# Stages between the Mamba scans merged into one stage by groups of four sequences, and the same for combine, norm and feed-forward

## What is computed

```python
def _mamba(x, wi, cw, cb, xpw, dw, db, Alog, Dp, wo):
    xin, z = jnp.split(jnp.einsum('bld,ed->ble', x, wi), 2, axis=-1)
    u = _silu(cb + sum((xpad[:, k:k + Ls, :] * cw[:, k] for k in range(4))))
    dt_in, Bc, Cc = split(jnp.einsum('blc,ec->ble', u, xpw))
    dt = jax.nn.softplus(jnp.einsum('blr,cr->blc', dt_in, dw) + db)
    ys = scan over 128 steps of h = exp(dt * A) * h + dt * u * B, y = h . C
    return jnp.einsum('blc,dc->bld', (ys + u * Dp) * _silu(z), wo)
for i in range(3):
    m = _layernorm(m + _mamba(m, ...), ln_g[i], ln_b[i])
moe_out = mix + shared
ff_out = silu(layer_norm(moe_out) @ ff_w1 + ff_b1) @ ff_w2 + ff_b2
return x + moe_out + ff_out
```

## Time and profile before

| | us |
|---|---|
| median of 3 runs (range) | 2821.89 (2815.56 to 2823.41) |
| the profiled execution, its own time | 2814.15 |
| its span | 2812.4 |
| recurrent input to the first scan | 1395.4 to 1496.2 |
| between first and second scan | 1721.1 to 1837.3 |
| between second and third scan | 2083.7 to 2198.9 |
| first mixture's combine and feed-forward | 1292.6 to 1395.4 |
| second mixture's combine and store | 2758.4 to 2812.4 |

### The profile page before, as it was taken

The page is one execution under the profiler, slowest core; times in us unless marked ns, Lnnn a source line. Parts: engine busy times, 40 slices in busy tenths (PEclk is TensorE's granted clock), DMA queues, the critical chain, the costliest instruction groups (busy, mean ns, idle before and its releaser), DMA issues. The chain is left out here.

```text
span 2812.4 us, 41657 instructions
## 1 busy us (share of the span) xinstructions
PE 2147.7 (76%) x14854; PEld 1446.1 (51%) x14854; DVE 1501.0 (53%) x3212; ACT 960.3 (34%) x2233; POOL 1185.5 (42%) x1118
## 2 busy tenths in 40 slices
PE   6999967999999756793645776389985699954791
PEld 4666744677787644692411223155551455643450
DVE  2343348766653022121468995778866788633352
ACT  2211112344444311241254663545536355300110
POOL 3011114544445414004107994089960799613104
PEclk7655558999999765696768998689996799955896
DMA  5000011211111000481002220022210222100562
GB/s 204 0 0 0 0 42 19 45 32 32 32 32 43 17 6 28 117 225 51 21 4 66 81 74 28 2 70 74 71 35 4 57 71 73 42 7 18 154 194 60
DMA packets 195585, 149.64 MB, mean 53 GB/s; under 512 B 93095, under 2 KB 154867, under 8 KB 193826
## 3 DMA queue, kind: packets, MB, share of 16 engines
q1 hardware_dynamic: 190802, 138.49, 17.5%
q0 software_dynamic: 4608, 8.86, 1.1%
HBM read 108.68 MB, written 39.19 MB: 53 GB/s over the span
## 5 line engine op out<-in xcount | busy, mean ns | idle before, releaser
L1405 DVE TENSOR_TENSOR_SCAN mc_states<-psum,mc_dbu 128x512 f32<-128x512 f32 x384 | 459.4, 1217 | 47.4 <-issue 30.1
L1314 POOL TENSOR_TENSOR mc_hc<-mc_states,mc_c_sb 128x1024 f32<-128x1024 f32 x192 | 451.4, 2351 | 41.6 <-DVE mc_states L1405 36.0
L1443 PE MATMUL psum<-mc_hc,ident 128*128 128x512 f32 x768 | 411.9, 633 | 52.2 <-POOL mc_hc L1314 52.2
L1325 ACT ACTIVATE psum<-dt,a 128x508 f32<-128x508 f32 x384 | 261.7, 687 | 20.2 <-DVE mc_states L1405 19.2
L1304 POOL TENSOR_TENSOR mc_dbu<-dtu,mc_b_sb 128x512 f32<-128x512 f32 (+1 forms) x192 | 226.9, 1182 | 8.7 <-ACT mc_b_sb L1332 8.7
L594 POOL TENSOR_TENSOR fw_tmp<-zeros 128x30 f32<-128x30 f32 (+14 forms) x240 | 121.8, 507 | 256.5 <-DMA zeros<-fw_blocks 238.3
L1710 POOL DMA_INDIRECT c_y<-slots_y,slots x64 | 64.2, 1003 | 330.5 <-PEq L1705 311.6
L1443 PEld LDWEIGHTS psum<-mc_hc,ident 128*128 128x128 f32 x768 | 122.6, 191 | 116.8 <-POOL mc_hc L1314 75.0
L189 POOL TENSOR_TENSOR t_rstd<-t_var,neg_half 128x4 f32<-128x4 f32 x32 | 32.3, 1009 | 288.8 <-DVE t_var L51 288.8
L1426 PE MATMUL psum<-bc,select 96*128 96x256 bf16 (+1 forms) x192 | 52.3, 272 | 122.0 <-PEq L35 120.6
L598 POOL TENSOR_TENSOR zeros<-zeros,fw_tmp 128x30 f32<-128x30 f32 (+14 forms) x240 | 133.5, 556 | 18.8
(11 more groups left out here) (387 smaller groups left out, 4676.5 us busy)
## 6 DMA issues: line engine op xcount, KB each, us to landing
mc_c_sb<-c_rows SPq DMA_DIRECT2D x192, 256.0 KB, 3.2
e_w<-in_L_ffn_ew SPq DMA_DIRECT2D x64, 256.0 KB, 3.3
slots_x<-zeros SPq DMA_DIRECT2D x12, 1024.0 KB, 12.7
e_x<-slots_x SPq DMA_DIRECT2D x96, 128.0 KB, 2.3
slots_y<-e_y SPq DMA_DIRECT2D x96, 128.0 KB, 1.9
e_w<-in_L_ffn_w SPq DMA_DIRECT2D x64, 128.0 KB, 2.2
fw_blocks<-fw_A SPq DMA_DIRECT2D x128, 32.0 KB, 1.7
zeros<-fw_blocks SPq DMA_DIRECT2D x8, 512.0 KB, 3.8
```

Source lines behind the costliest of these rows:

```text
L1314: nc.gpsimd.tensor_tensor(hc[:, k % 2], states[:, k % 2], c_sb[:, k % AHEAD, :].unsqueeze(1).to_broadcast([P, HALVES, GT]), ALU.mult).then ...
L1325: nc.scalar.activation(decay4[:, f, :, 1:P], z["dt"][:, f, cols].rearrange("p (b t) -> p b t", b=GS)[:, :, 1:P], ACT.Exp, scale=z["a"][:, ...
L1405: nc.vector.tensor_tensor_scan(out=states[:, k % 2, f, :], data0=decay_ps[:, f, :], data1=dbu[:, k % 2, f, :], initial=0.0, op0=ALU.mult, ...
L1443: last = nc.tensor.matmul(y_ps[:, f, :], m.ident, hc[:, k % 2, f, :], start=False, stop=(n == NSTATE - 1), skip_group_check=True)
```

## The change

`mamba_front_stage` takes the place of the input and step size stages, of the recurrent input stage in layer 0, and of the output stage of the layer before in layers 1 and 2. One block now does, group after group and with groups overlapped: output matmuls, norm, transpose, input matmuls, convolution, projection, split and step sizes. The normalised value is written by ScalarE (`normal`, scale and shift) and not by VectorE; the convolution reads the matmul result in PSUM, latest tap first, so `mi_xpad` and its copies are gone; the bf16 high part is written by ScalarE; softplus runs per group of 2 x 512 columns, not per half of 2048; the C rows leave in four DMAs. Only the last layer keeps `mamba_output_stage`. `load_back` moves into the scan's SyncE order, and `dparam` moves from the back to the front loads. `combine_ffn_stage` gathers by group, both choices of a group together, and norms and multiplies each group as it comes. `combine_store_stage` combines by group and stores each group by a DMA of its own.

```diff
-def ffn_stage(nc, io, m, tag, w, src, dst, func, extra=()):
+def combine_ffn_stage(nc, io, m, x):
...
             @block.gpsimd
             def _(pool):
-                norm_pool(nc, pool, n, m, s, 0)
+                def root(g):
+                    pool.wait_ge(s["ln_var"], g + 1)
+                    nc.gpsimd.tensor_tensor(n["rstd"][:, g, :], n["var"][:, g, :], m.neg_half[:, 0:GS], ALU.pow).then_inc(s["ln_rstd"], 1)
+
+                for g in range(GROUPS):
+                    gather_group(nc, ys, io["slots1_y"], x["slots"], g, m.gathered1)
+                    if g > 0:
+                        root(g - 1)
+                root(GROUPS - 1)
...
-                for g in range(GROUPS):
+                def residual(g):
+
+                    nc.vector.tensor_tensor(m.h[:, seqs(g), :], m.h[:, seqs(g), :], x1[:, seqs(g), :], ALU.add).then_inc(s["extra_done"], 1)
+                    dve.wait_ge(s["extra_done"], g + 1)
+                    nc.vector.tensor_tensor(m.h[:, seqs(g), :], m.h[:, seqs(g), :], moe[:, seqs(g), :], ALU.add).then_inc(s["both_done"], 1)
...
+                def finish(g):
                     dve.wait_ge(s["down_mm"], g + 1)
+                    nc.vector.tensor_tensor(m.h[:, seqs(g), :], m.h[:, seqs(g), :], down_ps[g % 2], ALU.add).then_inc(s["down_done"], 1)
...
+                for g in range(GROUPS):
+                    combine_group(nc, dve, ys, x["weights"], moe, s, g, m.gathered1)
+                    dve.wait_ge(s["second_done"], g + 1)
+                    normalise_stats(nc, dve, moe[:, seqs(g), :], n["stats"][:, g], n["mom"][:, g], n["var"][:, g, :], s, g + 1)
+                    residual(g)
+                    if g > 0:
+                        normed(g - 1)
+                    if g > 1:
+                        finish(g - 2)
+                normed(GROUPS - 1)
+                finish(GROUPS - 2)
+                finish(GROUPS - 1)
                 dve.wait_ge(s["down_done"], GROUPS)
...
+def mamba_front_stage(nc, io, m, z, r, layer):
...
-                for dst, a in [(r["wih"][:, :, :], io["lstm_w_ih"]), (whh[:, :, :], io["lstm_w_hh"]), (bias[:, :, :], io["lstm_bias"])]:
-                    sp.dma_start(dst, a).then_inc(s["w_in"], 16)
+                if first:
...
             @block.gpsimd
             def _(pool):
+                def step_times_input(g):
+                    pool.wait_ge(s["dt_done"], g + 1)
+                    nc.gpsimd.tensor_tensor(z["dtu"][:, :, cols(g)], z["dt"][:, :, cols(g)], z["u"][:, :, cols(g)], ALU.mult).then_inc(s["dtu_done"], 1)
+
...
+                def logarithm(g):
+                    e = z["y"][:, :, cols(g)]
+                    act.wait_ge(s["x_done"], HALVES * (g + 1))
+                    nc.scalar.activation(e, z["dt"][:, :, cols(g)], ACT.Abs).then_inc(s["abs_done"], 1)
+                    act.wait_ge(s["abs_done"], g + 1)
+                    nc.scalar.activation(e, e, ACT.Exp, scale=-1.0).then_inc(s["e_done"], 1)
...
+                    act.wait_ge(s["e_done"], g + 1)
+                    if g >= 2:
+                        act.wait_ge(s["dt_done"], g - 1)
+                    nc.scalar.activation(ln[:, g % 2], e, ACT.Ln, bias=m.ones_col[:, 0:1]).then_inc(s["ln_done"], 1)
+                normal(0)
+                normal(1)
+                turned(0)
+                turned(1)
+                gate(0)
+                channels(0)
+                normal(2)
+                projected(0)
+                gate(1)
+                turned(2)
+                step_input(0, 0)
+                channels(1)
+                gate(2)
+                normal(3)
+                projected(1)
+                turned(3)
+                step_input(0, 1)
+                logarithm(0)
+                channels(2)
+                gate(3)
+                step_input(1, 0)
+                channels(3)
+                step_input(1, 1)
+                projected(2)
+                logarithm(1)
+                step_input(2, 0)
+                projected(3)
+                step_input(2, 1)
+                logarithm(2)
+                step_input(3, 0)
+                step_input(3, 1)
+                logarithm(3)
...
+                def convolve(g):
+                    dve.wait_ge(s["in_mm"], 4 * g + HALVES)
...
+                        for f in range(HALVES):
+                            x = in_ps[f].rearrange("p (j c) -> p j c", j=GS)
+                            if late == 0:
+                                last = nc.vector.tensor_scalar(conv[:, g % 2, f], x, z["cw"][:, f, k:k + 1], z["cb"][:, f:f + 1], ALU.mult, ALU.add)
...
+                                last = nc.vector.scalar_tensor_tensor(out=to, in0=x[:, :, 0:P - late], scalar=z["cw"][:, f, k:k + 1], in1=to,
+                                                                      op0=ALU.mult, op1=ALU.add)
...
+                def step_size(g):
+
+                    e, w, l, x = z["y"][:, :, cols(g)], z["dtu"][:, :, cols(g)], ln[:, g % 2], z["dt"][:, :, cols(g)]
+                    dve.wait_ge(s["e_done"], g + 1)
+                    nc.vector.tensor_scalar(w, e, 1.0, -1.0, ALU.add, ALU.add).then_inc(s["w_done"], 1)
+                    dve.wait_ge(s["w_done"], g + 1)
+                    dve.wait_ge(s["ln_done"], g + 1)
+                    nc.vector.tensor_tensor(e, w, e, ALU.subtract).then_inc(s["diff_done"], 1)
+                    nc.vector.scalar_tensor_tensor(out=l, in0=w, scalar=0.0, in1=l, op0=ALU.is_gt, op1=ALU.mult).then_inc(s["masked_done"], 1)
+                    dve.wait_ge(s["masked_done"], g + 1)
+                    dve.wait_ge(s["diff_done"], g + 1)
+                    nc.vector.tensor_tensor(l, l, e, ALU.subtract).then_inc(s["t_done"], 1)
+                    dve.wait_ge(s["t_done"], g + 1)
+                    nc.vector.scalar_tensor_tensor(out=x, in0=x, scalar=0.0, in1=l, op0=ALU.max, op1=ALU.add).then_inc(s["dt_done"], 1)
+                dve.wait_ge(m.front_loaded, FRONT_LOADS * (layer + 1))
+                statistics(0)
+                statistics(1)
+                mean_shift(0)
+                mean_shift(1)
...
+                convolve(0)
+                statistics(2)
+                statistics(3)
+                mean_shift(2)
+                convolve(1)
+                split(0)
+                mean_shift(3)
+                convolve(2)
+                split(1)
+                convolve(3)
+                step_size(0)
+                split(2)
+                step_size(1)
+                split(3)
+                step_size(2)
...
+                dve.wait_ge(s["a_exp"], 1)
+                nc.vector.tensor_scalar(z["a"][:, :, :], z["a"][:, :, :], -1.0, None, ALU.mult).then_inc(s["a_done"], 1)
+                step_size(3)
...
...
                     sp.dma_start(c_sb[:, k % AHEAD, :], c_rows[n:n + 1, cols].to_broadcast([P, GT])).then_inc(c_in[k % AHEAD], 16)
+                    if k == AHEAD:
+                        load_back(sp, io, m, z, layer)
                     if k == NSTATE and layer < 2:
+                        sp.wait_ge(s["diag_done"], 2)
                         load_front(sp, io, m, z, layer + 1)
...
-                dve.wait_ge(m.back_loaded, BACK_LOADS * (layer + 1))
...
-            recurrent_input_stage(nc, io, m, z, r)
             for layer in range(3):
-                src = m.xT if layer == 0 else m.mT
-                mamba_input_stage(nc, io, m, z, layer, src)
-                mamba_step_size_stage(nc, io, m, z, layer)
+                mamba_front_stage(nc, io, m, z, r, layer)
                 mamba_scan_stage(nc, io, m, z, r, layer)
-                mamba_output_stage(nc, io, m, z, layer, src)
+            mamba_output_stage(nc, io, m, z, 2, m.mT)
...
+def combine_store_stage(nc, io, m, x):
...
+                for g in range(GROUPS):
+                    gather_group(nc, ys, io["slots2_y"], x["slots"], g, m.gathered2)
...
+                for g in range(GROUPS):
+                    combine_group(nc, dve, ys, x["weights"], m.h, s, g, m.gathered2)
+
+            @block.sync
+            def _(sp):
+                for g in range(GROUPS):
+                    sp.wait_ge(s["second_done"], g + 1)
+                    seqs = slice(GS * g, GS * (g + 1))
+                    sp.dma_start(io["out"][seqs].rearrange("b t d -> t b d"), m.h[:, seqs, :]).then_inc(s["stored"], 16)
+                sp.wait_ge(s["stored"], 16 * GROUPS)
```

532 lines of the change are left out of this document (273 added, 259 removed).

## The result

The changed kernel takes **2733.36 us** (median), the kernel before 2819.88 beside it: a ratio of 0.9693, 95% interval 0.9662 to 0.9723. The forecast was 2742, with a range of 2718 to 2775. One of its four executions took 2833.66, in a slower state of the chip that executions of any kernel can fall into; the ratio leaves such executions out. The profiled execution took 2733.23 with a span of 2731.2, so 81.2 less span than before, where the sum had 75.7.

A forecast was written before the change was run, and what follows sets the result against it. No engine fills the stretch between scans: stages stand in a row, each bound by one engine while others wait. Gains of 20.7, 19.7, 8.7, 23.5 and 3.1 total 75.7, giving 2738.5 or 2746.2 us; middle 2742, range 2718 to 2775.

The forecast's parts named there:

- head, to the first convolution: New stage, layers 1 and 2: first output matmul through statistics, normalisation, transposes and two input matmuls to first convolution, 17.8 us.
- two convolutions: New stage, layers 1 and 2: two convolutions and the VectorE work between them, 15.0 us; 14 to 18 by PSUM price.
- from there to group 3's logarithm: New stage, layers 1 and 2: ScalarE sets the pace, 34.7 us, including 5.8 of waits for half-clock TensorE.
- taps from PSUM: Convolution on VectorE: first two taps rise from 0.50 to 0.69 us each reading PSUM, six stay; 5.8 per group.
- Rival 1: Second half of the new stage: TensorE keeps full clock, 5.8 us of waits go per layer, 17.4 in all, 2725; chance 0.20.
- Layer 0: Layer 0's new stage: 92.2 us against 100.9, gain 8.7, including 6.4 until the loads have landed.
- Combine and feed-forward: First mixture's combine and feed-forward by groups: stage ends at 1371.9 where 1395.4 stood, gain 23.5 us.
- The end: Last combine and store: landing 1.3 us later, sums of 2.15, last store only 256 KB; gain 3.1.
- Costed at nothing: Zero cost for `load_back` in the scan's SyncE order, C rows in four parts, and roots on GpSimd.
- Rival 2: GpSimd's products delay VectorE's two-input operations: 6.75 us a layer, 20.2 in all, 2762; chance 0.14.
- Rival 3: ScalarE: each table switch costs 1.38 us more, nine on the path in three layers, 37 in all, 2779; chance 0.03.
- Rivals 4 and 5: Whole kernel: TensorE's clock never rises, 2830 us, chance 0.03; or groups stay chained without overlap, 2822, chance 0.02.

The follow-up runs named there:

- second profile: The changed kernel run once more, unaltered; median 2704.58 us, ratio 0.9664 to the kernel before beside it.
- second bank: Changed kernel with the second half of a group's step inputs in a PSUM bank of its own, groups 1 to 3; ratio 0.965 to the kernel before.
- moving the product: Group 2's product dt times u on VectorE too, added to a kernel combining several follow-up edits of the changed kernel; 2706.47 us, ratio 0.9607 to the kernel before.
- added switches: Changed kernel with three more table switches per layer, an unused one-column SiLU between Exp and Ln of groups 1 to 3; ratio 0.9717 to the kernel before.
- the last product: Changed kernel with group 3's product dt times u on VectorE instead of GpSimd; ratio 0.9702 to the kernel before.

## Why the prediction was right

The time came out 9 us below the forecast and the path held step by step. That the number is so near is in part luck. The gaps and the end gained 12.7 more than forecast (3.5, 2.0, 3.3 and 3.9), the first profile's feed-forward 6.8 less, in an execution in which TensorE was late, and the code that doesn't change took 0.4 more: 81.2 against 75.7. In the second profile, whose feed-forward ran undisturbed, the five stretches gained 88.9. In the second layer the steps were:

| step | forecast | measured |
|---|---|---|
| end of scan to first output matmul | 2.45 | 2.60 |
| head, to the first convolution | 17.8 | 17.1 |
| two convolutions | 15.0 | 14.6 |
| to group 0's logarithm | 15.0 | 14.4 |
| from there to group 3's logarithm | 34.7 | 33.8 |
| VectorE's and GpSimd's tail | 7.3 | 7.4 |
| 40 semaphores | 3.3 | 3.6 |
| sum | 95.5 | 93.5 |

Each step was right to within 1 us. The four long ones were forecast 0.4 to 0.9 too long, the three short ones 0.1 to 0.3 too short; that makes the 2.0 by which this gain was undersized. In the third layer it was 3.3, with a shorter head (16.3) in code that is the same. The taps from PSUM cost what was put: 1.53 for the first pair, 4.25 for six. ScalarE waited for 3.27 and 2.22 in its part, 5.7 with a small one, for 5.8 forecast. The reason given, half clock, is only part of it. The matmul ahead of the wait of 2.22 took 2.04 where 1.09 is usual at full clock, so the clock accounts for about 1; the rest is that it had to wait until ScalarE had read the one PSUM bank, since with a second bank the wait is gone, though the last of these matmuls still takes 2.04. Rival 1 fell: the clock was at 0.56 there.

*Layer 0*: 3.5 undersized. The wait for loads was 5.1 and not 6.4 (the last load was issued 3.2 after the first, not 4.1, and landed 1.8 later, not 2.3), the head 9.6, not 10.7, and ScalarE's part 33.3, not 34.5.

*Combine and feed-forward*: the term was 23.5 and the code gives 23.8 (the feed-forward by itself) and 24.0 (the second profile: 79 with the 5 of loads taken off); the first profile's 16.7 was an execution in which TensorE's results came 2.5 late and its clock fell. The working was right in its parts: first transposes at 28.1 after the first gather (27.8), 14.4 and 11.4 per group (13.6 and 11.0 in the second profile). Where it was short: the root stands behind the gathers of the next group was seen, but not that moving it is worth 9.8.

*The end*: the term that failed, 3.1 forecast and 7.0 measured. It is also added up wrongly: 1.3 later, sums 2.1 shorter and a landing 1.7 shorter make 2.5, not 3.1. The wrong step is that I carried the stall of one gather over to shorter bursts, as three stalls of 0.95; there was none. The last rows landed 41.3 after the first gather, not 43.1 as before: 1.8 earlier where I had 1.3 later. And the last store, with its issue, took 3.36 to the end of the span where the terms leave 4.9 (2806.65 - 2805.78 = 0.87 to its issue, 3.3 to land and 0.75 behind it).

*Costed at nothing*: rightly. The scans' gain or loss is not from the moved loads: the first scan took 224.8 to 228.2 in kernels with the moved loads and without them alike, 228.1 in two that have the scan of before unaltered. The same holds for the 3.7 ahead of the first gather.

Rival 2 was half right. The collision of GpSimd's products with VectorE's two-input operations was there but lay beside the path; the second bank put it on it, and moving the product took it off (1.22 for 2.40). By the Trainium skill ("SBUF — State Buffer", SBUF: two separate sides) one blocks the other for the whole instruction, and these rows agree: the operation ended 1.08 after GpSimd's product had (1738.74 + 2.81 = 1741.55 and 1742.63), nearly its whole usual length of 1.23. Rival 3, by the Trainium skill ("ScalarE: Activation LUTs", What ACT_TABLE_LOAD costs), is refuted by the added switches: 1.28 each and no drain. Rivals 4 and 5 did not occur.

## What to carry to other kernels

Stages joined by groups gain what the engines waited for each other, and such a gain can be forecast step by step from the durations of the old stages, if the new path is walked through engine by engine; what is moved to save a switch or a wait must be charged with what the new order costs elsewhere, the waits and a longer tail above all. Once the path is bound by one engine's chain, look at what is queued ahead of the first item of the next stage: a root placed four gathers earlier gave 10 us, nearly as much as all edits of the three long stages together (11.5). And judge a change of 1% by stretches of the trace as well as by whole times, and a change of 1 us by the one step that the edit touches: the gaps alone called the last product half a miss, its tail shows 1.15 in each.

## What was not expected of the hardware

Code that no kernel changes took 1262 to 1293 us from the start to the first gather in different executions, and the first scan 224.8 to 228.2: more than most edits here are worth. In three of the eleven executions with the grouped feed-forward it was 5 to 7 us longer than in the others; in two of them TensorE's rows have 0.7 to 1.8 us of standing between matmuls that had nothing to wait for, followed by a group at 1.2 GHz.

The head of the front stage, unchanged in most kernels here, took 14.9 to 17.3 in the third gap. Part of it is the clock that TensorE brings along: where it took 14.9, the first output matmuls ran at 2.4 GHz at once (0.68 for four), where it took 16.3 they began at 1.2 GHz (1.20).

And the gather that was held beside sixteen sums ended 0.8 after the last of them in all six cases; beside eight with a wait after four, and sixteen with a wait after eight, none was held.
